# Routed experts of a transformer block: 63 blocks of 128 rows against 48 pairs of 64-row halves on two column tiles of TensorE

## The reference, cut to what matters

```python
logits = x @ gate_w
probs = jax.nn.softmax(logits, axis=-1)
topw, topi = jax.lax.top_k(probs, K)
topw = topw / jnp.sum(topw, axis=-1, keepdims=True)
combine = jnp.zeros((T, E), x.dtype).at[jnp.arange(T)[:, None], topi].set(topw)
def body(acc, ew):
    wg_e, wu_e, wd_e, c_e = ew
    h = jax.nn.silu(x @ wg_e) * (x @ wu_e)
    return (acc + c_e[:, None] * (h @ wd_e), None)
out, _ = jax.lax.scan(body, jnp.zeros_like(x), (wg, wu, wd, combine.T))
```

## Time and profile before

| | us |
|---|---|
| median of three runs | 610.32 |
| the three runs | 610.14, 610.32, 612.68 |
| the profiled execution | 612.54 |
| its span, first to last instruction | 610.8 |
| busy: PE, PEld | 460.5, 342.7 |
| busy: DVE, ACT, POOL | 376.5, 267.7, 230.9 |
| mean granted clock of TensorE | 0.872 |

### The profile page before, as it was taken

The page is one execution under the profiler, slowest core; times in us unless marked ns, Lnnn a source line. Parts: engine busy times, 40 slices in busy tenths (PEclk is TensorE's granted clock), DMA queues, the critical chain, the costliest instruction groups (busy, mean ns, idle before and its releaser), DMA issues.

```text
span 610.8 us, 9971 instructions
## 1 busy us (share of the span) xinstructions
PE 460.5 (75%) x3201; PEld 342.7 (56%) x3201; DVE 376.5 (62%) x936; ACT 267.7 (44%) x514; POOL 230.9 (38%) x309
## 2 busy tenths in 40 slices
PE   2766888988887669697985163768779699999935
PEld 1644444544443348586765042557568588878834
DVE  6584576777663255836578865976363466666626
ACT  7416666666567433133732064151432245444412
POOL 5950234333456420502400402036427166656610
PEclk9957599999789769998996776789699799999969
DMA  7590341011410039800000000999202355454263
GB/s 198 147 185 23 65 67 40 25 42 37 139 49 6 8 107 339 247 2 1 0 2 0 26 26 26 193 255 273 70 32 104 94 158 147 132 141 130 61 222 123
DMA packets 56083, 60.17 MB, mean 99 GB/s; under 512 B 10452, under 2 KB 46941, under 8 KB 56032
## 3 DMA queue, kind: packets, MB, share of 16 engines
q1 hardware_dynamic: 50864, 50.79, 31.7%
q0 software_dynamic: 5168, 8.74, 4.3%
HBM read 37.67 MB, written 25.75 MB: 104 GB/s over the span
## 4 chain that ended last, share of the span: by engine, by line
PE 42%; DVE 22%; issue 14%; POOL 10%; ACT 10%; DMA 2%; SPq 0%; POOLq 0%; DVEq 0%; ACTq 0%
PE ps L1877 6%; PE ps L2133 5%; PE ps L1856 5%; PE ps L1835 4%; POOL x_sorted_scratch L791 4%; ACT probs L1548 4%; POOL y_slots_scratch L816 3%; PE ps L1927 3%; PE ps L2152 3%; PE ps L1915 2%; PE ps L1916 2%; PE ps L1917 2%; DVE st L908 2%; PE ps L1889 2%; DVE gain L1108 2%
## 5 line engine op out<-in xcount | busy, mean ns | idle before, releaser
L1548 ACT ACTIVATE probs<-ps 128x512 f32<-128x512 f32 x160 | 86.8, 595 | 58.2 <-PE ps L1856 56.4
L1002 DVE TENSOR_REDUCE negm<-ps 128x2 f32<-128x1024 f32 (+1 forms) x64 | 67.0, 1080 | 24.7 <-PE ps L1845 24.4
L816 POOL DMA_INDIRECT y_slots_scratch<-yblk,ids x63 | 61.9, 983 | 48.2 <-issue 32.4
L660 POOL TENSOR_TENSOR rstd<-ve,halfneg 128x4 f32<-128x4 f32 x15 | 15.3, 1023 | 123.3 <-DVE ve L937 57.0
L2133 PE MATMUL ps<-wgu,xcol 128*128 x252 | 58.4, 355 | 1.2 <-issue 0.5
L1835 PE MATMUL ps<-k_all,q_ring 64*128 64x512 f32 (+3 forms) x256 | 52.6, 419 | 8.2 <-DVE negm L1002 4.9
L1856 PE MATMUL ps<-q_ring,k_all 64*128 64x512 f32 (+3 forms) x256 | 43.6, 400 | 17.7 <-ACT probs L1548 17.7
L1877 PE MATMUL ps<-probs,v_all 128*32 128x128 f32 (+3 forms) x512 | 49.2, 484 | 5.9 <-DVE att L1030 3.1
L1588 ACT CAST h_hi<-hf 128x512 fp32r<-128x512 f32 x28 | 17.4, 620 | 65.9 <-DVE hf L1060 65.9
L2133 PEld LDWEIGHTS ps<-wgu,xcol 128*128 128x128 f32 x252 | 40.3, 193 | 9.2 <-issue 6.3
L1856 PEld LDWEIGHTS ps<-q_ring,k_all 64*128 64x128 f32 x256 | 23.1, 208 | 39.0 <-ACT probs L1548 31.0
(11 more groups left out here) (306 smaller groups left out, 1304.0 us busy)
## 6 DMA issues: line engine op xcount, KB each, us to landing
x_sorted_scratch<-pad SPq DMA_DIRECT2D x7, 1206.0 KB, 13.3
xblk<-x_sorted_scratch SPq DMA_DIRECT2D x63, 134.0 KB, 2.2
wgu<-in_moe_w SPq DMA_DIRECT2D x4, 1536.0 KB, 16.2
q_ring<-q_parts_scratch SPq DMA_DIRECT2D x64, 64.0 KB
ycomb<-y_slots_scratch SPq DMA_DIRECT2D x8, 512.0 KB, 7.4
wd<-in_moe_w SPq DMA_DIRECT2D x1, 3072.0 KB, 19.8
sraw<-in_moe_w SPq DMA_DIRECT2D x6, 384.0 KB, 3.4
q_parts_scratch<-qparts SPq DMA_DIRECT2D x4, 512.0 KB, 4.7
```

The lines of the kernel that those rows point to most:

```text
L816: pool.indirect_dma_start(out=y_slots, out_offset=bass.IndirectOffsetOnAxis(ap=ids[:, i:i + 1], axis=0), in_=yblk[:, i % YR, :], in_offset ...
L1002: dve.tensor_reduce(negm[:, par, :, hp, qt], pair_of, AX.X, ALU.max, negate=True).then_inc(s1_read, 1)
L1548: act.activation(probs[:, par, u, :], ps[:, col_unit(g, u), :], ACT.Exp)\
```

## The change

The routed stage works on half blocks of `HB` = 64 rows. Each expert owns one half, whether or not it fills it; what does not fit goes to "free" halves, in order of experts, of which there can be `FREE` = 64. The 32 + 64 halves make `BLOCKS` = 48 pairs. In every three pairs ("trio") the first has free half 3c and own half 2c, the second free half 3c+1 and own half 2c+1, the third two free halves (3c+2 and 48+c). So the expert of a second half is fixed in the code in two of three pairs. The last pair is taken as one block of one expert.

TensorE's up and down products are split by halves: the first half's 64 columns go to PSUM partitions 0 to 63, the second's to 64 to 127, two column tiles of the array, each with its own expert's weights. Transposes stay whole. ScalarE copies the weights of the second free half of a trio's third pair to `wcopy` and `wdcopy`, two buffers each, so that TensorE needs one register a pair. TensorE's registers are loaded four at a time. In TensorE's turn the order is now transposes of `i`, hidden transpose of `i - 3`, up product of `i - 1`, down product of `i - 4`; VectorE and ScalarE are moved to match. Waits that others imply are left out. SyncE loads a pair with two DMAs. `route_places` works out the new places with 15 limits and some more steps. The core of the diff:

```diff
-BLOCKS = N * TOPK // P + E - 1
+HB = P // 2
+LIMITS = N // HB - 1
+FREE = N * TOPK // HB
+BLOCKS = (E + FREE) // 2
+TRIOS = BLOCKS // 3
...
+        def own_expert(i):
+            return None if i % 3 == 2 else i // 3 * 2 + i % 3
+        def first_rows(i):
+            own = own_expert(i)
+            return E * HB + i * HB, (E + BLOCKS + i // 3) * HB if own is None else own * HB
...
-                sp.dma_start(xblk[:, i % XR, :], x_sorted[i * P:(i + 1) * P, :])\
-                    .then_inc(xb_in[i % XR], 16)
+                for n, first in enumerate(first_rows(i)):
+                    sp.dma_start(xblk[half(n), i % XR, :], x_sorted[first:first + HB, :])\
+                        .then_inc(xb_in[i % XR], 16)
...
+            pool.iota(placi[:, BLOCKS:2 * BLOCKS].rearrange("p (g m) -> p g m", m=3),
+                      [[2 * HB, TRIOS], [HB, 3]], base=0, channel_multiplier=1)\
...
+            def to_own(rank):
+                chain.step(dve.scalar_tensor_tensor(
+                    pos[:, :, :], rank, float(HB),
+                    own[:, :].unsqueeze(1).to_broadcast((P, TPB, E)), ALU.is_lt, ALU.mult))
...
-                    over[:, :, :], total.unsqueeze(2).to_broadcast((P, E, 8)),
-                    thr[:, :].unsqueeze(1).to_broadcast((P, E, 8)), ALU.is_gt))
+                    over[:, :, :], total.unsqueeze(2).to_broadcast((P, E, LIMITS)),
+                    thr[:, :].unsqueeze(1).to_broadcast((P, E, LIMITS)), ALU.is_gt))
                 if b == 1:
...
+                    to_own(rank)
...
+                    chain.step(dve.scalar_tensor_tensor(
+                        ex0[:, :], in0[:, :], float(E - 1), nb0[:, :], ALU.add, ALU.subtract))
+                    chain.settle()
+                    chain.step(dve.tensor_tensor(own[:, :], iota[:, :], ex0[:, :], ALU.subtract))
+                    chain.settle()
+                    to_own(rank)
+                    chain.settle()
+                    chain.step(dve.tensor_tensor(
+                        late[:, :, :], pos[:, :, :], ex0[:, :].unsqueeze(1).to_broadcast(grid),
+                        ALU.add))
...
+                    chain.step(dve.tensor_tensor(late[:, :, :], late[:, :, :], pos[:, :, :],
+                                                 ALU.add))
...
-            for i in range(BLOCKS + 2):
+            for i in range(BLOCKS + 3):
                 if i < BLOCKS:
                     block_in(i)
-                if 0 <= i - 1 < BLOCKS:
-                    block_gate(i - 1)
+                if 0 <= i - 3 < BLOCKS:
+                    block_hidden(i - 3)
+                if 0 <= i - 2 < BLOCKS:
+                    block_gate(i - 2)
                 if i < BLOCKS:
                     block_ids(i)
-                if 0 <= i - 2 < BLOCKS:
-                    block_hidden(i - 2)
...
+            def copy_weights(c, e):
+                act.copy(wcopy[:, c % 2, :, :, :], wgu[:, :, :, bass.ds(e * F, F)])
+                act.copy(wdcopy[0:F, c % 2, :],
+                         wd[0:F, bass.ds(e, 1), :].rearrange("p o d -> p (o d)"))\
+                    .then_inc(w_copied, 1)
...
+            for i in range(BLOCKS + 4):
+                if i % 8 == 1 and 8 <= i <= 41:
                     diagonal(*diagonals[i // 8 - 1])
-                if i < BLOCKS:
-                    block_silu(i)
-                if i >= 2:
-                    block_out(i - 2)
+                if 0 <= i - 1 < BLOCKS:
+                    block_silu(i - 1)
+                if 0 <= i - 4 < BLOCKS:
+                    block_out(i - 4)
+                c = i // 3
+                if i % 3 == 0 and c < TRIOS - 1:
+                    copy_weights(c, act.value_load(etab[0:1, BLOCKS + c:BLOCKS + c + 1],
+                                                   min_val=0, max_val=E - 1))
...
+                own, c = own_expert(i), i // 3
                 pe.wait_ge(bt_copied, i + 1)
-                if i >= 2:
-                    pe.wait_ge(b_mul, i - 1)
+                if own is None and c < TRIOS - 1:
+                    pe.wait_ge(w_copied, c + 1)
                 for k in range(DC):
...
+                    if i == BLOCKS - 1:
+                        mm = pe.matmul(up, cols, free, start=k == 0, stop=k == DC - 1)
+                    else:
+                        second = (wcopy[:, c % 2, k, :, :] if own is None
+                                  else wgu[:, k, :, own * F:(own + 1) * F])
+                        pe.matmul(up[half(0)], cols[:, half(0)], free, start=k == 0,
+                                  stop=k == DC - 1)
+                        mm = pe.matmul(up[half(1)], cols[:, half(1)], second, start=k == 0,
+                                       stop=k == DC - 1)
...
+                    pe.matmul(ps[half(0), 4 + i % 2, 0:D], hcol[0:F, i % 2, half(0)], free,
+                              start=True, stop=True)
+                    mm = pe.matmul(ps[half(1), 4 + i % 2, 0:D], hcol[0:F, i % 2, half(1)],
+                                   wdcopy[0:F, c % 2, :] if own is None else wd[0:F, own, :],
+                                   start=True, stop=True)
...
-            for i in range(BLOCKS + 3):
+            for i in range(BLOCKS + 4):
                 if i < BLOCKS:
                     block_in(i)
+                    if i % 4 == 0:
+                        _, loaded = nc.values_load_multi_w_load_instructions(
+                            etab[0:1, i:i + 4], engines=[mybir.EngineType.PE], min_val=0,
+                            max_val=E - 1)
+                        experts.update(enumerate(loaded, i))
+                if 0 <= i - 3 < BLOCKS:
+                    block_hidden(i - 3)
                 if 0 <= i - 1 < BLOCKS:
-                    experts[i - 1] = pe.value_load(etab[0:1, i - 1:i], min_val=0, max_val=E - 1)
                     block_up(i - 1, experts[i - 1])
-                if 0 <= i - 2 < BLOCKS:
-                    block_hidden(i - 2)
-                if 0 <= i - 3 < BLOCKS:
-                    block_down(i - 3, experts.pop(i - 3))
+                if 0 <= i - 4 < BLOCKS:
+                    block_down(i - 4, experts.pop(i - 4))
```

More of the change, by code:

```diff
@@ L210, in sandwich_kernel @@
             ("eq", [P, TPB, TOPK, E], F32), ("mask", [P, TILES, E], BF16))
-        (nb0, nb1, in0, in1, ex0, jump, lim0, onesE, pos, late, destf, dest), end = place(
+        (nb0, nb1, in0, in1, ex0, jump, lim0, own, onesE, pos, late, destf, dest), end = place(
             end, ("nb0", [P, E], F32), ("nb1", [P, E], F32),
             ("in0", [P, E], F32), ("in1", [P, E], F32), ("ex0", [P, E], F32),
-            ("jump", [P, E], F32), ("lim0", [P, E], F32), ("onesE", [P, E], F32),
+            ("jump", [P, E], F32), ("lim0", [P, E], F32), ("own", [P, E], F32), ("onesE", [P, E], F32),
             ("pos", [P, TPB, E], F32), ("late", [P, TPB, E], F32),
@@ L576, in _ @@
             sp.wait_ge(s_pad, 3)
-            for n in range(7):
+            for n in range(6):
                 sp.dma_start(
-                    x_sorted[n * 9 * P:(n + 1) * 9 * P, :].rearrange("(b p) f -> p b f", p=P),
-                    pad[:, :].unsqueeze(1).to_broadcast((P, 9, XW))).then_inc(s_sorted, 16)
+                    x_sorted[n * 8 * P:(n + 1) * 8 * P, :].rearrange("(b p) f -> p b f", p=P),
+                    pad[:, :].unsqueeze(1).to_broadcast((P, 8, XW))).then_inc(s_sorted, 16)
             def load_chunk(c):
@@ L1214, in block_constants @@
             def block_constants():
-                dve.wait_ge(s_const2, 6)
+                dve.wait_ge(s_const2, 7)
                 chain.step(dve.memset(rows[:, :, D + TOPK:XW], 0.0))
-                chain.step(dve.tensor_copy(placf[:, :], placi[:, :]))
+                chain.step(dve.tensor_scalar(placf[half(0), :], placi[half(0), 0:BLOCKS],
+                                             float(E * HB), None, ALU.add))
+                second = placf[half(1), :].rearrange("p (g m) -> p g m", m=3)
+                chain.step(dve.tensor_scalar(
+                    second[:, :, 0:2],
+                    placi[half(1), BLOCKS:].rearrange("p (g m) -> p g m", m=3)[:, :, 0:2],
+                    float(-HB), None, ALU.add))
+                chain.step(dve.tensor_scalar(second[:, :, 2], placi[half(1), 0:TRIOS],
+                                             float((E + BLOCKS - 1) * HB), None, ALU.add))
                 chain.settle()
@@ L1274, in route_places @@
                     chain.settle()
-                    chain.step(dve.scalar_tensor_tensor(
-                        pos[:, :, :], late[:, :, :], float(P), rank, ALU.mult, ALU.add))
+                    chain.step(dve.tensor_tensor(late[:, :, :], late[:, :, :], pos[:, :, :],
+                                                 ALU.add))
+                chain.settle()
+                chain.step(dve.scalar_tensor_tensor(
+                    pos[:, :, :], late[:, :, :], float(HB), rank, ALU.mult, ALU.add))
                 chain.settle()
```

70 lines of the change are left out of this document (38 added, 32 removed).

## The result

| | before | after |
|---|---|---|
| median of the runs made together, us | 611.50 (4 runs) | 601.88 (4 runs) |
| lowest to highest, us | 610.14 to 613.34 | 600.61 to 602.62 |
| the profiled execution, us | 612.54 | 600.61 |
| its span, us | 610.8 | 598.8 |
| mean granted clock of TensorE | 0.872 | 0.856 |

The ratio is 0.9839, with a 95% interval of 0.9801 to 0.9876: faster by 1.6%. 602.3 us was forecast. The sum behind that number was less good than the number: one term is 5.3 us off, and others take some of it back.

A forecast was written before the change was run, and what follows sets the result against it. TensorE was taken to bound the routed stage. Terms -11.9 (stage), +1.3 (end), +2.3 (places) and +0.3 (first load) gave -8.0 us: 604.5 from the profiled 612.54, less 2.2 to the median, 602.3 us; range 590 to 615.

The forecast's parts named there:

- The count and the columns: Routed stage: 48 pairs for 63 blocks, streamed columns a pair T and H 0.32, U 0.64, D 0.43 us.
- The overlap of the halves: Up and down products: two column tiles of 64 run entirely side by side, as L1877's four of 32 do.
- rival 4: Up and down products: the two tiles don't run side by side at all; period 2.89, 652.6 us; chance 0.05.
- rival 2: Up and down products: tiles only half overlap, +0.21 us a pair, 612.2 us; chance 0.10.
- The changes of tiling: TensorE, two switches a pair between full array and half-wide tiles: 0.165 us each, 0.33 a pair.
- Rival 1: Routed stage: switches nearly free and loads hidden; period 1.56, 588.8 us; chance 0.13.
- The register loads: TensorE's sequencer, four expert numbers every fourth pair: 0.10 us a pair taken, 0 and 0.44 kept as bounds.
- my own line: Stall a pair: 0.5 us until the loads are reached, plus loads and checks, less 1.93 until H, over four.
- Rival 3: TensorE's sequencer: four loads in a row at 0.63 us, mostly exposed; period 2.16, 618.3 us; chance 0.14.
- The deferral: D deferred to four periods: gives H, hidden copy and gate a period each, costs a period at the end.
- Ahead of the stage: New places and first load before the routed stage: batch 0 +1.3, batch 1 +1.0, second half load +0.3 us.
- The end: Last transpose to last scatter's end: four D's, not three, follow the last T, scatters at 1.29 us: +1.3 us.

The follow-up runs named there:

- The run with one half: The changed kernel with the second half's up and down products left out: 602.49 us, ratio 0.9823 to the kernel before.
- the run with the short deferral: The changed kernel with hidden transpose and down product both two periods behind the input transposes: 615.61 us, ratio 1.003 to the kernel before.
- the full-width run: The changed kernel with all 48 pairs' up and down products at full width, using the first half's expert: 596.52 us, ratio 0.9725 to the kernel before.
- the old blocks in the new order: The kernel before, 63 blocks and old places, with the changed kernel's order, deferral, fewer waits and loads of four: 611.84 us, ratio 0.9982.

## Why the prediction was right, and where it was not

T, H, U and D are the input transposes, the hidden transpose, the up and the down product.

**The count and the columns.** Right. 48 pairs; T and H 0.21 and 0.11, U 0.64, D 0.43. Without changes of tiling a period is 1.42 us where the streamed columns gave 1.39.

**The overlap of the halves.** Right, and read from the right rows: L1877's four tiles of 32 in the attention foretold two tiles of 64. The run with one half settles it, and with it rival 4. Of rival 2, the Trainium skill's "TensorE: Matmul & The Clock Gate", The mechanism, has matmuls start and end in program order. The trace agrees as far as it goes: the starts of the halves alternate, first half, second half, 0.01 us apart, and never cross. What the rival needed besides, both passes of one half ahead of the other's, does not show: passes are 0.16 us apart, in twos.

**The changes of tiling.** Right in kind, slightly dear. 0.165 us was taken, two ways of measuring give 0.147 and 0.143. The three gaps of 0.15 in the earlier trace rows were the price itself; what I added for the first weight load was not needed. In the period above one sees where it lies: the first instruction of the new tiling starts 0.09 us late (0.20 from H to U for 0.11) and the one behind it another 0.05 (0.21 for 0.16). On the way back the first transpose starts 0.10 us late (0.53 for 0.43) and the second another 0.06 (0.28 from T to H for 0.22). The Trainium skill, "TensorEngine Tiling (Array Packing)", Key Properties, speaks of a drain there; the rows agree, with 0.145 us. Rival 1 falls.

**The register loads.** This is the step that failed. It put 0.10 us a pair, "near the median load"; measured is next to nothing, and 47 x 0.10 is 4.7 of the 5.3 us by which the stage came out shorter. The other 0.6 are small: 47 x 0.035 less for the changes of tiling and 0.25 less for the first pairs, against 47 x 0.03 more for the columns. Two sizes in the term of the loads were wrong, and in opposite directions: four numbers come with one load of 0.33 us, not four of 0.30, but a check takes 0.28, not the 0.17 taken from the register operation's own duration in the earlier trace rows. Together 1.45 us, between my 0.98 and 1.88, and with that size my own line gives (0.5 + 1.45 - 1.93)/4 = 0.01 us. The 0.5 us after T at which the sequencer reaches the loads was only an estimate: it is 0.2 to 0.5 in the kernel after, mostly 0.45 to 0.65 at a period of 1.42, and 1.4 in the run with the short deferral. At a period of 1.42 the same line gives a stall of 0.3 us, and 0.5 to 0.6 was measured: there H is at least 0.35 us late, and in the full-width run U another 0.13 behind it (521.06 to 521.30 for 0.11). The count of dropped waits was wrong too: "four or five waits a block" are three in the diff, and the sequencer's own semaphore instructions go from 4.1 a block to 1.3 a pair. Rival 3 was this same burst; its mechanism exists, as the full-width run and the old blocks in the new order show, but its end of four long loads does not.

**The deferral.** I gave it one sentence and no price, since beside TensorE "none of the rest is late". The run with the short deferral says that with two periods for both this sentence would have failed by 0.4 us a pair, 18.9 us of the transposes' span (99.9 for 81.0). The cover was there as I said, but its worth was not in my sum, because the forecast started from the streaming and not from the old loop's waits.

**Ahead of the stage.** Batch 1: 1.0 us forecast, and 6.45 for 5.45 us from `over` to the first scatter, 1.00, in all the kernels with the new places. Batch 0: I took all of "0 to 1.3"; the length was right (1.35), but in seven of eight profiles nearly nothing of it arrives. The first load: 0.3 us was taken from the issue of a whole block. The second half goes out 0.57 us after the first, and the first one itself follows the start of the last scatter by 2.9 us for 2.4 to 2.6 (475.32 to 478.24 above, against the earlier trace rows), in all the kernels with the new loads; why is open. The scatters take 0.3 less. From the first scatter of batch 1 to the first transpose it is 25.8 to 26.2 us for 25.1 or 25.2, so 0.75 and not 0.3. With batch 0 it makes some +3.1 of the +3.6; the rest lies before batch 0's places, where the two executions are 0.6 apart (388.0 and 387.4).

**The end.** One period of scatters more, +1.5 for +1.3.

So the forecast's -8.0 stands against -11.9 in the two profiled executions and -9.6 in the medians. I had taken off another 2.2 us, the distance between the profiled execution of before and the median; but the profiled execution of after lies 1.3 below its own median. So the 3.9 us that the sum fell short were made up by 2.2 + 1.3 = 3.5 us that have nothing to do with the change. That the number came out 0.4 us off is luck, and the range, not the number, was what the working could carry.

**Where the gain is from.** By the spans of the transposes: the new order on the old blocks, 98.2 to 96.2; 48 blocks for 63 in that order, 96.2 to 74.3; two changes of tiling a pair, 74.3 to 81.0, of which 47 x 0.295 = 13.9 are their price and 7 come back because the longer period hides the checks (the 7 is the difference; full-width pairs without checks were not run). Of the 17.2 us, 5 go ahead of and behind the stage. On the old blocks the checks alone hold back 96.2 - 87.9 = 8.3 us of the span, 6.9 by the medians (611.84 and 604.91). The pairs bring about as much net: 9.6 for the change less the 2 for its order.

## What to carry to other kernels

Count changes of tiling like instructions: group the work so that a loop has few of them, and weigh each against the blocks that the tiles save. Before a rework of the tiles, look at what the bounding engine's sequencer does between its instructions: a burst of register loads and checks costs nothing while the sequencer reaches it early enough to be through before the next instruction is wanted. Here it was hidden at a period of 1.71 us, cost 0.5 us at 1.42, and cost 0.5 us again at 1.95 where the sequencer came to it late. A deferral by some periods pays if a consumer would otherwise stand in the open, and its price is at the end: 9.4 us from the last transpose to the last scatter here, 7.3 with the short deferral.

## What the runs showed of the hardware that was not expected

- A load of four registers takes 0.33 us, one of a single register 0.30.
- A bounds check occupies TensorE's sequencer for about 0.28 us, though its operations are listed with 0.15 and 0.02.
- SyncE takes 0.44 us to issue a load of 64 rows by itself and 0.60 us for one right behind another, 0.32 and 0.43 us for one of 128 rows, of the same length each. So a pair costs 0.44 + 0.60 = 1.04 us of issue, a whole block 0.32.
- A change between full and half tiles costs 0.147 or 0.143 us, whether a period has two of them or four (1.42, 1.71 and 2.00 us with none, two and four).
- Half of a pair's products can be left out without changing the time by 0.01 us a pair.
